# Masks in one transfer, queries ahead of a key third, later key parts and heads by one product in a cross attention kernel

## The reference

```python
B, S, L, NL, D, H = 16, 56, 1500, 6, 128, 16      # HD = 8
def _attn(q, k, v, mask):
    scores = einsum('bqhd,bkhd->bhqk', q, k) / sqrt(HD)
    scores = where(mask[:, None, None, :], -inf, scores)
    return einsum('bhqk,bkhd->bqhd', softmax(scores), v)
for i in range(NL):
    xn = _adaln(x, cond, n1_w[i], n1_b[i])
    q, k, v = split(xn @ qkv_w[i].T)               # self attention, 56 keys
    x = x + _attn(_rope(q), _rope(k), v, src_mask) @ so_w[i].T
    xn = _adaln(x, cond, n2_w[i], n2_b[i])
    q = _rope(xn @ cq_w[i].T)                      # cross attention, 1500 keys
    k, v = _rope(ctx @ ck_w[i].T), ctx @ cv_w[i].T
    x = x + _attn(q, k, v, ctx_mask) @ co_w[i].T
    xn = _adaln(x, cond, n3_w[i], n3_b[i])
    x = x + gelu(xn @ f1_w[i].T + f1_b[i]) @ f2_w[i].T + f2_b[i]
```

## Time and profile before

| | |
|---|---|
| median of 3 runs | 6056.02 us (6052.6 to 6056.93) |
| profiled execution, its own time | 6043.84 us |
| its span from first to last instruction | 6042.0 us |
| busy share over the span | PE 93%, PEld 69%, DVE 63%, ACT 53%, POOL 37% |
| block 0's slots | 181 to 2963 us |

### The profile page before, as it was taken

The page is one execution under the profiler, slowest core; times in us unless marked ns, Lnnn a source line. Parts: engine busy times, 40 slices in busy tenths (PEclk is TensorE's granted clock), DMA queues, the critical chain, the costliest instruction groups (busy, mean ns, idle before and its releaser), DMA issues.

```text
span 6042.0 us, 140669 instructions
## 1 busy us (share of the span) xinstructions
PE 5595.8 (93%) x55893; PEld 4177.1 (69%) x55893; DVE 3779.0 (63%) x8627; ACT 3230.0 (53%) x6405; POOL 2247.7 (37%) x2204
## 2 busy tenths in 40 slices
PE   5899999999999999999799999998799999989997
PEld 4667667677676676776457778776477777756984
DVE  3888888887887888888553444444544444444553
ACT  1566666666766766667543344443333333324764
POOL 4666666666666666656200000000011111156440
PEclk7999999999999999999898999999799999998998
DMA  2776776776767767768400100001000000030000
GB/s 63 120 118 106 119 120 104 120 116 107 125 110 115 121 109 116 121 107 130 92 11 10 42 32 32 30 29 33 11 11 16 11 16 11 11 105 24 1 1 25
DMA packets 396485, 407.85 MB, mean 68 GB/s; under 512 B 125575, under 2 KB 372946, under 8 KB 393786
## 3 DMA queue, kind: packets, MB, share of 16 engines
q1 hardware_dynamic: 395834, 398.85, 37.6%
HBM read 158.00 MB, written 0.46 MB: 26 GB/s over the span
## 4 chain that ended last, share of the span: by engine, by line
PE 62%; POOL 8%; SPq 7%; DVE 7%; issue 7%; ACT 5%; DMA 3%; POOLq 1%; DVEq 0%; ACTq 0%
PE psum L2276 11%; PE psum L2243 10%; PE psum L1575 5%; PE psum L1587 4%; PE psum L2288 4%; PE psum L1561 4%; SPq L1475 4%; POOL slot_context L3476 3%; PE psum L1723 2%; PE psum L1609 2%; PE psum L1601 2%; SPq L1493 2%; PE psum L416 2%; PE psum L430 2%; DVE row_max L1940 2%
## 5 line engine op out<-in xcount | busy, mean ns | idle before, releaser
L1940 DVE TENSOR_REDUCE row_max<-psum 112x1 f32<-112x500 f32 x2304 | 1443.3, 670 | 185.2 <-PE psum L1575 170.4
L2067 ACT ACTIVATE weights<-psum 125x448 f32<-125x448 f32 x2304 | 1140.8, 541 | 521.2 <-PE psum L1561 514.6
L1575 PE MATMUL psum<-key_stack,query_stack 97*128 97x500 bf16 x2304 | 874.6, 380 | 111.0 <-DMA query_stack<-query_parts 51.1
L1561 PEld LDWEIGHTS psum<-query_stack,key_stack 121*128 121x128 bf16 x9216 | 654.1, 99 | 370.9 <-issue 184.6
L1561 PE MATMUL psum<-query_stack,key_stack 121*128 121x112 bf16 x9216 | 837.6, 213 | 33.2 <-ACT weights L2067 27.9
L2356 DVE TENSOR_REDUCE l_stat<-psum 128x1 f32<-128x1500 f32 (+1 forms) x224 | 391.7, 1749 | 544.9 <-PE psum L2243 544.9
L2276 PE MATMUL psum<-l_ctx_v,l_turned 125*128 125x128 f32 x5376 | 713.7, 281 | 16.4 <-ACT l_turned L2314 12.2
L2276 PEld LDWEIGHTS psum<-l_ctx_v,l_turned 125*128 125x128 f32 x5376 | 643.1, 191 | 59.2 <-ACT l_turned L2314 40.2
L1587 PE MATMUL psum<-weights,values 125*17 125x112 f32 x18432 | 553.9, 261 | 0.0
L1587 PEld LDWEIGHTS psum<-weights,values 125*17 125x17 f32 x18432 | 408.0, 97 | 144.1 <-issue 141.2
L2314 ACT ACTIVATE l_turned<-psum 125x512 f32<-125x512 f32 x448 | 251.3, 597 | 434.9 <-PE psum L2288 432.1
(11 more groups left out here) (539 smaller groups left out, 10182.9 us busy)
## 6 DMA issues: line engine op xcount, KB each, us to landing
key_stack<-key_parts SPq DMA_DIRECT2D x1728, 125.0 KB, 4.6
ctx_t<-in_ctxT SPq DMA_DIRECT2D x96, 750.0 KB
l_ctx_v<-in_ctxV SPq DMA_DIRECT2D x32, 750.0 KB
query_stack<-query_parts SPq DMA_DIRECT2D x576, 28.0 KB, 3.5
l_ctx_t<-in_ctxT SPq DMA_DIRECT2D x16, 750.0 KB
slot_context<-in_ctxV SPq DMA_DIRECT2D x16, 750.0 KB
key_stack<-ctx_mask_rows SPq DMA_DIRECT2D x576, 3.9 KB
sm_w<-in_sm_w SPq DMA_DIRECT2D x3, 2048.0 KB
```

What stands on the lines that cost most here:

```text
L1561: mm = e.matmul(self.k.psum[:, h, (p % 4) * QC:(p % 4 + 1) * QC], ks[:, at:at + 128], q[:, p * QC:(p + 1) * QC])
L1575: e.matmul(self.k.psum[:, 2 + n % 2, 0:500], q[0:ROWS_MAX, p * QC:p * QC + 128], ks[0:ROWS_MAX, p, c * 500:(c + 1) * 500]).then_inc(self.m ...
L1940: e.tensor_reduce(self.largest[:, i % PAIRS, i // PAIRS:i // PAIRS + 1], k.psum[0:QC, 2 + i % 2, 0:500], AX.X, ALU.max, negate=True).then_ ...
L2067: e.activation(half(self.p[kt % RING_P], h), self.k.psum[0:KN, h, 0:HALF], ACT.Exp).then_inc(self.exped.sem, 1)
```

## The change

It does six things. (1) The masks lie as 16 rows of 1500, and a slot sends one transfer of 1x8x1500. (2) SyncE issues the queries ahead of key third 1. (3) `key_temp` has two buffers, and VectorE waits for the third part of the key third two before. (4) ScalarE makes first parts at ticks 3, 7 and 11 and second parts at 4, 8 and 0. (5) GpSimd's remainder is at `late` 3 and its third part at `late` 4, taken first. (6) The sums are transposed to columns 0, 120, 256 and 376, so that all 16 heads lie 32 apart, and `divide` multiplies them by one instruction.

```diff
-            self.mask_rows = sb("ctx_mask_rows", [6 * B, L // 6], BF16)[:, :]
+            self.mask_rows = sb("ctx_mask_rows", [B, L], BF16)[:, :]
...
-            self.tm = sb("key_temp", [128, 2, 500])
+            self.tm = [sb(f"key_temp{i}", [128, 2, 500]) for i in range(2)]
...
-        self.mask_stacked = ev("key_mask_stacked", NS, step=96)
+        self.mask_stacked = ev("key_mask_stacked", NS, step=16)
...
-            for n in range(6):
-                e.dma_start(dst[ROWS:ROWS + 1, :, n * 250:(n + 1) * 250],
-                            self.mask_rows[6 * b + n:6 * b + n + 1, :].unsqueeze(1).broadcast_to(
-                                [1, PAIRS, 250])).then_inc(self.mask_stacked.sem, 16)
+            e.dma_start(dst[ROWS:ROWS + 1, :, :],
+                        self.mask_rows[b:b + 1, :].unsqueeze(1).broadcast_to([1, PAIRS, L])).then_inc(
+                            self.mask_stacked.sem, 16)
...
             if 0 <= s + 2 < NS:
+                self.stack_queries(e, s + 2)
                 self.stack_keys(e, s + 2, 1)
...
             if 0 <= s + 2 < NS:
-                self.stack_queries(e, s + 2)
                 self.stack_keys(e, s + 2, 2)
...
-                tr = e.transpose(side.bank(*key)[0:S, i * 128:(i + 1) * 128], self.acc[:, i * S:(i + 1) * S],
-                                 k.ident[:, :])
+                at = i * 128 - 8 * (i % 2)
+                tr = e.transpose(side.bank(*key)[0:S, at:at + 128], self.acc[:, i * S:(i + 1) * S], k.ident[:, :])
...
-        for g in range(2):
-            for h2 in range(2):
-                v = blocks[:, g, 128 * h2:128 * (h2 + 1)].rearrange("p (j c) -> p j c", j=4)[:, :, 1 + 8 * h2:9 + 8 * h2]
-                m = 2 * g + h2
-                op = e.tensor_tensor(o[:, m * 32:(m + 1) * 32].rearrange("p (j d) -> p j d", j=4), v,
-                                     spread(inv[:, 4 * m:4 * m + 4], 8), ALU.mult)
+        e.tensor_tensor(o.rearrange("p (m d) -> p m d", d=8), bk.rearrange("p (m c) -> p m c", c=32)[:, :, 1:9],
+                        spread(inv, 8), ALU.mult).then_inc(side.emptied(*key), 1)
...
-            if (b, c) > (0, 0):
-                e.wait_ge(self.key_lo.sem, self.key_lo(b, c) - 1)
+            if (b, c) > (0, 1):
+                e.wait_ge(self.key_lo.sem, self.key_lo(b, c) - 2)
...
-        hi = {2: (s + 2, 1), 6: (s + 2, 2), 10: (s + 3, 0)}.get(kt)
-        mid = {3: (s + 2, 1), 7: (s + 2, 2), 11: (s + 3, 0)}.get(kt)
+        hi = {3: (s + 2, 1), 7: (s + 2, 2), 11: (s + 3, 0)}.get(kt)
+        mid = {4: (s + 2, 1), 8: (s + 2, 2), 0: (s + 2, 0)}.get(kt)
...
-        for late in range(1, 4):
+        for late in (4, 3, 1):
...
-            if late == 2:
+            if late == 3:
...
-            if late == 3:
+            if late == 4:
```

More of the change, by code:

```diff
@@ L1313, in __init__ @@
                 self.src_mask8 = k.sb(s2, "src_mask8", [1, T], U8)[:, :]
-                self.ctx_mask8 = k.sb(s2, "ctx_mask8", [6 * B, L // 6], U8)[:, :]
+                self.ctx_mask8 = k.sb(s2, "ctx_mask8", [B, L], U8)[:, :]
         self.tables_arrived = ev("l0_tables_arrived", step=112)
@@ L1509, in sync @@
         e.dma_start(self.parity, dr["head_parity"]).then_inc(sem, 16)
-        e.dma_start(self.ctx_mask8, dr["ctx_mask"]).then_inc(sem, 16)
+        e.dma_start(self.ctx_mask8, dr["ctx_mask"].rearrange("(b n) c -> b (n c)", b=B)).then_inc(sem, 16)
         e.dma_start(self.bias[:, :, :], dr["l0_bias"]).then_inc(sem, 16)
@@ L1739, in phase_tensor @@
                 for m in range(4):
-                    tr = e.transpose(side.bank(*key)[0:S, m * 128:(m + 1) * 128], self.sacc[:, m * S:(m + 1) * S],
-                                     k.ident[:, :])
+                    at = m * 128 - 8 * (m % 2)
+                    tr = e.transpose(side.bank(*key)[0:S, at:at + 128], self.sacc[:, m * S:(m + 1) * S], k.ident[:, :])
                 tr.then_inc(side.filled, 1)
@@ L1817, in fixed_vector @@
             e.wait_ge(side.filled, side.at(*key))
-            if (b, c) > (0, 0):
-                e.wait_ge(self.key_lo.sem, self.key_lo(b, c) - 1)
-            bk = side.bank(*key)[:, 0:500]
-            e.stream_shuffle(self.tm[:, 1, :], bk, OTHER_HALF).then_inc(self.key_turned.sem, 1)
-            e.tensor_tensor(self.tm[:, 0, :], bk, self.cos[:, cols], ALU.mult).then_inc(side.emptied(*key), 1)
+            if (b, c) > (0, 1):
+                e.wait_ge(self.key_lo.sem, self.key_lo(b, c) - 2)
+            bk, tm = side.bank(*key)[:, 0:500], self.tm[(3 * b + c) % 2]
+            e.stream_shuffle(tm[:, 1, :], bk, OTHER_HALF).then_inc(self.key_turned.sem, 1)
+            e.tensor_tensor(tm[:, 0, :], bk, self.cos[:, cols], ALU.mult).then_inc(side.emptied(*key), 1)
         if 1 <= s <= NS and kt == 2:
@@ L1965, in fixed_scalar @@
                 e.wait_ge(self.part_stacked[n % 2].sem, self.part_stacked[n % 2](n // 2 - 1))
-            e.activation(self.k_part[n % 2][:, 0, :], self.tm[:, 0, :], ACT.Copy).then_inc(self.key_hi.sem, 1)
+            e.activation(self.k_part[n % 2][:, 0, :], self.tm[n % 2][:, 0, :], ACT.Copy).then_inc(self.key_hi.sem, 1)
         if mid and 0 <= mid[0] < NS:
@@ L1969, in fixed_scalar @@
             e.wait_ge(self.key_rest.sem, self.key_rest(b, c))
-            e.activation(self.k_part[(3 * b + c) % 2][:, 1, :], self.tm[:, 1, :], ACT.Copy).then_inc(self.key_mid.sem, 1)
+            e.activation(self.k_part[(3 * b + c) % 2][:, 1, :], self.tm[(3 * b + c) % 2][:, 1, :], ACT.Copy).then_inc(self.key_mid.sem, 1)
         if 0 <= s + 2 < NS and kt == 2:
@@ L2074, in key_gpsimd @@
     def key_gpsimd(self, e, s, kt):
-        tm, side = self.tm, self.side
-        for late in range(1, 4):
+        side = self.side
+        for late in (4, 3, 1):
             if kt < late:
@@ L2083, in key_gpsimd @@
             b, c = at
-            part = self.k_part[(3 * b + c) % 2]
+            part, tm = self.k_part[(3 * b + c) % 2], self.tm[(3 * b + c) % 2]
             if late == 1:
```

6 lines of the change are left out of this document (2 added, 4 removed).

## The result

The changed kernel takes 6115.26 us, median of 4 runs (6108.77 to 6116.73), against 6054.31 for the kernel before in the same comparison: ratio 1.0098, 95% interval 1.0081 to 1.0116, so 49 to 70 us slower. The forecast of no change was wrong, and the time lies above its range (6016 to 6092).

What follows compares the result with a forecast made beforehand. The prediction took TensorE as the bound, its matmuls busy 2629 of 2767 us. Terms -48 - 9 - 5 + 1 - 7 + 43 + 21 + 4 sum to 0, so 6056 us; 8 in 10 between 6016 and 6092.

Steps and rivals of the forecast that it cites:

- The queries' waits: TensorE's waits for query transfers behind key third 1 on SP: all but some 3 us go, -48 us.
- Slots begin 4.9 us earlier: At the start, one mask transfer and the new order bring the first queries forward some 7 us: -5 us.
- `l_qd`: Self-attention ticks: GpSimd's third part delays rotation, the blocked query and TensorE's matmul behind it, +43 us.
- One product: VectorE's four products dividing the heads become one, at most 0.36 us less, covered by slack: 0.
- two `key_temp`: VectorE's 20.7 us of waiting for GpSimd's third key part go; a third counts as time: -7 us.
- Key parts have two buffers still: ScalarE's first part waits 1.1 to 1.5 us for key third 1's landing; TensorE loses 0.8 in 26 slots: +21 us.
- the +4 for the context fetch: The context fetch behind the later third 2 pushes the next key third 0: +4 us, between 0 and 20.
- buffer wait at full price: Rival, chance 0.12: ScalarE's wait for key transfers passes whole to TensorE, third 0 comes late: 6073 to 6100 us.
- the clock, -9: Half-clock stretches, together 20.4 us, go with the query waits; about half of that is regained: -9 us.
- One mask transfer, 0 in the steady slots: SP saves 3.4 us of mask issues, but the queries are ready later anyway in the light slot: 0.
- Later parts, "0, at best -15": ScalarE's parts no longer wait for GpSimd's rotation, but VectorE's turned key lasts longer still: 0, at best -15 us.
- Is TensorE full?: TensorE taken as full, so the 43 us delay is lost; if not, it is absorbed, 6013 us (rival, chance 0.20).

Runs made afterwards that it cites:

- the third buffer: The changed kernel with three key_parts buffers in place of two, so ScalarE's first part waits for the third three before: 6057.48 us, ratio 1.0010.
- the small edits: The kernel before with one mask transfer, two key_temp and one product for the heads, queries and parts left as they were: 6019.00 us, ratio 0.9943.
- both repairs and old ticks: The changed kernel with three key_parts buffers, l_qd ahead of GpSimd's key steps, and key parts at their old ticks: 5999.29 us, ratio 0.9911.

## Why the prediction was wrong

**Held.** The queries' waits went, -48. Slots begin 4.9 us earlier, -5. `l_qd` was forecast at +43 in some 60 waits: it is 42.9 us in 66, and moving it gave 54. (The sum as written there, 33 times 1.0 and 44 times 0.2, is 42.) One product was put at 0 and two `key_temp` at -7; each measures 3 gained, and the interval holds both forecasts.

Two terms failed, and they overlap: the buffers and the clock.

**The first step that failed: "Key parts have two buffers still ... +21".** The mechanism was the right one and stood there; its size was not. With the +4 for the context fetch it was 25 us, and the third buffer gives 53 back, 41 of them waiting. Three things were short.
- *The landing.* I took 3.2 us to the last issue and 4.6 to landing, 7.8 together. In the slot shown it is 9.7: SyncE's issues take 5.02 us, which the earlier trace rows showed for that same key third (5.01). As a rule it is 8.7, the median over 96 slots, and it was 8.7 in the kernel before too: the median landing of one transfer is not that of the last of six.
- *The slots.* 40 of the 57 waits and 102 of the 121.6 us are in third 0's first part, 2.6 us each and not 1.3. In each phase three slots have it, not two: the last two and the first of the next. The other waits are in the thirds behind it, which I left out.
- *Slack.* I gave TensorE 0.5 us and took 0.8 a slot. By start times the scores inside slots are 66 us later.

The rival "buffer wait at full price" was the case. Its price for the buffers, 17 to 45 over the forecast, holds the measured 28; that the time lies above its 6073 to 6100 comes from the clock, below, and from the busy time that is not explained.

**The second step that failed: the clock, -9.** I took away the half clock with the query waits, but the new waits bring 68 us of it in place of 26, about +21 instead of -9. The term had to be worked out from the waits left, not from the ones taken away. Of this, 12 us are in the 53 above.

**One mask transfer, 0 in the steady slots.** Alone it is 21 us. I looked at one slot and found SyncE's time covered there; in a third of the slots it is not, and key third 1 and the queries stood behind the masks. This likely kept the miss from being larger.

**Later parts, "0, at best -15".** Of TensorE's 27.9 us for exponentials 7.3 are left once the third buffer is there, so 21 did go. I had named VectorE as what lasts longer, and it does, one slot later. The four combinations of the two moves, with the small edits in all, show what each does (medians; by their ratios 0.9943 and 1.0208, 1.0060 and 1.0098):

| | parts at old ticks | later parts |
|---|---|---|
| queries behind third 1 | 6019.00 | 6179.00 |
| queries ahead | 6088.20 | 6115.26 |

With two buffers no move gets below the small edits alone, and what one is worth hangs on the other: the queries ahead cost 71 us at old ticks and gain 67 with later parts, where the queries behind third 1 are waited for 113.6 us. With the third buffer at old ticks the moved queries come out 11 us under the small edits alone (0.9925 against 0.9943), which is within the intervals, and 19 with `l_qd` first (0.9911), which is not.

**Is TensorE full?** It has no slack to make up a delay here: 43 us of waits at L1718 came back as 54 when they were taken away. The 31% that the weight loads' busy share leaves absorbed nothing. The Trainium skill (Perfetto Trace Analysis, Identifying the Most-Contended Engine) says that the matmuls' busy share does not tell how close TensorE is to its roofline, and names the matmul work done against the peak and the weight loads' busy share for that. That is another question, and the prediction's reading of it, that 31% to spare would absorb the delay, was not borne out; whether a delay comes back as time was told by matmul records that stand end on start.

**Left open.** How many of the us come through the clock was read from stretches and busy times and not tried by itself, and half of the 43 us of busy time are not explained. The small edits together gain 35 us and one by one 21, 3 and 3, with intervals of 7 us each way; whether the rest is more than that was not tried.

## What to carry to other kernels

When a transfer is moved ahead of another, follow the buffer that the other one holds, to its landing, and ask who writes to it next and what stands behind that writer; take the time from the first issue of the same set to its last landing, over all slots. A repair that takes a wait away is worth its time only up to the next engine's limit, here VectorE's rope, and a wait of 2 us moved there can still cost clock. Small transfers that nobody waits for still take the issuing engine's time, and one slot in which it is covered does not speak for the others.

## What the runs showed of the hardware

SyncE's six issues of a key third take 3.8 us (at 1371.10) or 5.0 (at 1381.97). For key third 1 they lie between 3.8 and 5.7 us over the 96 slots, with a median of 3.9 before and 3.8 in the changed kernel; what lengthens some is not shown. The last of the six has landed 8.7 us after the first issue by the median in both kernels, 7.7 to 10.0 at the ends. Six mask transfers of 250 columns take SyncE 4.07 us, one of 1500 takes 0.70. One row of the changed kernel, TensorE's timeline:

```profile
1213.50 0.37 PE L1574 MATMUL psum<-key_stack,query_stack 97*128 97x500 bf16 x1 [1.96 <-DMA key_stack<-key_parts]
```

TensorE's clock fell to 1.2 GHz for 3.4 to 10.2 us beside single waits (this one, then 10.2 us at 0.51 from 1214.9, in the table at the top). In the changed kernel twelve of the fifteen stretches stand beside waits of 1.9 to 2.9 us and three beside waits of 1.2 to 1.4, while seven waits of 1.9 us or more passed without one. So the length of the wait alone does not decide. In the kernel with both repairs and old ticks, whose steady waits are at most 1.4 us, it never fell between 181 and 2924 us.
